# The last feed-forward tile's quantisation in two column parts, and VectorE's order in the drain

## The reference

```python
        def mx_qdq(x, s_bits=S_BITS, e_bits=E_BITS, group=GROUP):
            ...
            amax = jnp.max(jnp.abs(xg), axis=-1, keepdims=True)
            shared_exp = jnp.floor(jnp.log2(jnp.maximum(amax, tiny))) - bias
            scale = jnp.exp2(shared_exp)
            xs = xg / scale
            ...
            dq = (q * scale).reshape(shp)
        ...
        g = mx_linear(x, w_gate)
        u = mx_linear(x, w_up)
        return mx_linear(jax.nn.silu(g) * u, w_down)
```

## Time and profile before

| | |
|---|---|
| median of three runs | 700.44 us |
| the profiled execution | 700.79 us |
| its span, first to last instruction | 698.8 us |
| TensorE matmuls busy | 649.1 us (93%) |
| VectorE busy | 587.8 us (84%) |
| ScalarE busy | 509.0 us (73%) |
| GpSimd busy | 502.4 us (72%) |

### The profile page before, as it was taken

How to read it: one execution, slowest core, us unless ns; L and a number is a source line. 1 busy time by engine, 2 the same in 40 slices (tenths; PEclk the granted TensorE clock), 3 DMA queues, 4 the chain that set the end, 5 groups by cost and what they waited for, 6 DMA issues and landing times.

```text
span 698.8 us, 13988 instructions
## 1 busy us (share of the span) xinstructions
PE 649.1 (93%) x5188; PEld 340.7 (49%) x5200; DVE 587.8 (84%) x881; ACT 509.0 (73%) x969; POOL 502.4 (72%) x617
## 2 busy tenths in 40 slices
PE   0749899999999999999999999999999999999994
PEld 0749787354444443443443434434444454555542
DVE  3948977998788998988988989988889479999995
ACT  5244366878888797888888887987888756665665
POOL 1326456889898798898898987988786774767563
PEclk9857999999999999999999999999999999999999
DMA  9990202000000000001000000000000000000011
GB/s 310 163 259 21 63 3 75 1 15 17 16 16 1 32 17 15 31 1 31 31 1 31 31 1 32 4 27 28 1 13 1 1 1 1 31 30 31 32 46 75
DMA packets 21763, 26.91 MB, mean 39 GB/s; under 512 B 4032, under 2 KB 12224, under 8 KB 21696
## 3 DMA queue, kind: packets, MB, share of 16 engines
q1 hardware_dynamic: 21696, 26.02, 13.3%
HBM read 21.82 MB, written 4.19 MB: 37 GB/s over the span
## 4 chain that ended last, share of the span: by engine, by line
PE 77%; DVE 8%; issue 6%; POOL 4%; ACT 3%; DMA 2%; SPq 0%; POOLq 0%; ACTq 0%; DVEq 0%
PE banks L2470 9%; PE banks L2447 9%; PE banks L2437 9%; PE banks L2494 9%; PE banks L2480 9%; PE banks L2517 8%; PE banks L2551 7%; PE banks L2422 4%; PE banks L2578 3%; PE banks L2405 2%; PE banks L2525 2%; DMA big<-in_L_ffn_w_down_dram 2%; PE banks L2506 1%; DVE big L826 1%; PE banks L2458 1%
## 5 line engine op out<-in xcount | busy, mean ns | idle before, releaser
L1551 ACT ACTIVATE big<-banks 128x512 f32<-128x512 f32 (+3 forms) x352 | 196.6, 590 | 47.7 <-PE banks L2480 22.5
L541 POOL TENSOR_TENSOR big<-big 128x512 f32<-128x512 f32 x128 | 137.1, 1085 | 21.7 <-DVE big L931 21.6
L1621 ACT ACTIVATE big<-banks,big 128x512 f32<-128x512 f32 x128 | 87.8, 692 | 21.5 <-DVE big L911 21.4
L911 DVE TENSOR_REDUCE big<-banks 128x1 f32<-128x512 f32 x128 | 82.9, 680 | 18.2 <-PE banks L2437 16.9
L532 POOL TENSOR_TENSOR big<-big 128x512 f32<-128x512 f32 x64 | 82.2, 1285 | 15.1 <-ACT big L1626 14.8
L917 DVE TENSOR_REDUCE big<-banks 128x16 f32<-128x1024 f32 x64 | 77.4, 1209 | 17.8 <-PE banks L2447 17.4
L2470 PEld LDWEIGHTS banks<-ident,big 128*128 128x128 f32 x512 | 54.6, 141 | 76.6 <-issue 36.3
L922 DVE TENSOR_TENSOR big<-banks,big 128x1024 f32<-128x1024 f32 x64 | 78.1, 1221 | 5.5 <-PE banks L2480 3.8
L2480 PEld LDWEIGHTS banks<-ident,big 128*128 128x128 f32 x512 | 55.0, 141 | 54.2 <-ACT big L1551 28.0
L2470 PE MATMUL banks<-ident,big 128*128 128x128 f32 x512 | 79.5, 283 | 1.5 <-ACT big L1551 1.5
L2480 PE MATMUL banks<-ident,big 128*128 128x128 f32 x512 | 75.4, 282 | 0.4 <-ACT big L1551 0.3
(11 more groups left out here) (111 smaller groups left out, 1204.8 us busy)
## 6 DMA issues: line engine op xcount, KB each, us to landing
big<-in_x_dram SPq DMA_DIRECT2D x8, 1024.0 KB, 11.2
big<-in_ctx_dram SPq DMA_DIRECT2D x16, 256.0 KB, 2.9
out_dram<-big SPq DMA_DIRECT2D x16, 256.0 KB, 2.0
big<-in_L_ffn_w_down_dram SPq DMA_DIRECT2D x4, 688.0 KB, 12.0
big<-in_L_ffn_w_gate_dram SPq DMA_DIRECT2D x10, 256.0 KB, 2.7
big<-in_L_ffn_w_up_dram SPq DMA_DIRECT2D x10, 256.0 KB, 2.8
wg_area<-in_L_xattn_Wq_dram SPq DMA_DIRECT2D x2, 128.0 KB, 11.4
wg_area<-in_L_xattn_Wk_dram SPq DMA_DIRECT2D x2, 128.0 KB, 7.8
```

What stands on the lines that cost most here:

```text
L541: pool.tensor_tensor(e, e, r, ALU.mult).then_inc(s.p_ready, 1)
L911: dve.tensor_reduce(kneg[:, par, i:i + 1], bank[par], X, ALU.max, negate=True).then_inc(s.k_max_ready, 1)
L1551: return act.activation(dst, src, ACT.Copy)
L1621: act.activation(EK[:, f % 2, par, i], bank[par], ACT.Exp, bias=kneg[:, par, i:i + 1], accum_out=ksum[:, f % 2, par, i:i + 1]).then_inc(s. ...
```

## The change

The last tile (15) is quantised in two parts, columns 0 to 767 (24 groups) and 768 to 1375 (19 groups), the same cut as that of its transposes. The first part needs only two of the three column pieces of the hidden row, so its maximum is taken before the third is there. `transpose_h(15, 0)` waits for the first part alone. VectorE's list is written anew from `multiply_h(15, 1)` on.

```diff
+    LAST = [(0, 6 * P // GRP), (6 * P // GRP, FFN // GRP)]
...
+            def shift_last(r):
+                pool.wait_ge(s.h_inv_ready, T + r)
+                g0, g1 = LAST[r]
+                amax, inv, scale = (v[:, g0:g1] for v in hk[(T - 1) % 2])
+                group_scales(amax, inv, scale)
+                h = hs[:, (T - 1) % 4, GRP * g0:GRP * g1]
+                pool.tensor_tensor(groups(h), groups(h), spread(inv, g1 - g0), ALU.mult).then_inc(s.hy_ready, 1)
...
-            shift_hidden(T - 1)
+            shift_last(0)
+            shift_last(1)
...
+            def scale_last(r):
+                g0, g1 = LAST[r]
+                dve.wait_ge(s.h_ready, NC * (T - 1) + 2 + r)
...
+                dve.tensor_reduce(hk[(T - 1) % 2][0][:, g0:g1], groups(hs[:, (T - 1) % 4, GRP * g0:GRP * g1]), X, ALU.max,
+                                  apply_absolute_value=True).then_inc(s.h_max_ready, 1)
+
+            def mask_last(r):
+                g0, g1 = LAST[r]
+                dve.wait_ge(s.h_max_ready, T + r)
+                amax = hk[(T - 1) % 2][0][:, g0:g1].bitcast(I32)
+                dve.tensor_scalar(amax, amax, 0x7F800000, None, ALU.bitwise_and).then_inc(s.h_inv_ready, 1)
+
+            def clip_last(r):
+                g0, g1 = LAST[r]
+                dve.wait_ge(s.hy_ready, T + r)
+                dve.wait_ge(s.hq_ready, T - 1)
+                to_fp8(h8[:, GRP * g0:GRP * g1], hs[:, (T - 1) % 4, GRP * g0:GRP * g1]).then_inc(s.h_clipped, 1)
+
+            def dequant_last(r):
+                g0, g1 = LAST[r]
+                dve.wait_ge(s.h_clipped, T + r)
+                dve.wait_ge(s.tr_ready, tr_no[T - 3, "h1"] + 1)
+                dve.tensor_tensor(groups(hq[:, (T - 1) % 2, GRP * g0:GRP * g1]), groups(h8[:, GRP * g0:GRP * g1]),
+                                  spread(hk[(T - 1) % 2][2][:, g0:g1], g1 - g0), ALU.mult).then_inc(s.hq_ready, 1)
...
             multiply_h(T - 1, 1)
+            scale_last(0)
             add_down(T - 5)
+            mask_last(0)
             out_stats(T - 5)
             clip_hidden(T - 2)
             multiply_h(T - 1, 2)
-            scale_hidden(T - 1)
-            mask_hidden(T - 1)
+            scale_last(1)
+            mask_last(1)
             dequant_hidden(T - 2)
             add_down(T - 4)
+            clip_last(0)
+            dequant_last(0)
+            clip_last(1)
+            dequant_last(1)
+            add_down(T - 3)
             out_stats(T - 4)
-            add_down(T - 3)
-            clip_hidden(T - 1)
-            dequant_hidden(T - 1)
             out_stats(T - 3)
...
-                pe.wait_ge(s.hq_ready, u + 1)
+                pe.wait_ge(s.hq_ready, T + r if u == T - 1 else u + 1)
```

More of the change, by code:

```diff
@@ L1009, in dequant_hidden @@
                                   ).then_inc(s.hq_ready, 1)
+            def scale_last(r):
+                g0, g1 = LAST[r]
+                dve.wait_ge(s.h_ready, NC * (T - 1) + 2 + r)
+                dve.wait_ge(s.hy_ready, T - 2)
+                dve.wait_ge(s.hq_ready, T - 2)
+                dve.tensor_reduce(hk[(T - 1) % 2][0][:, g0:g1], groups(hs[:, (T - 1) % 4, GRP * g0:GRP * g1]), X, ALU.max,
[16 more added lines that the diff above has]
+                                  spread(hk[(T - 1) % 2][2][:, g0:g1], g1 - g0), ALU.mult).then_inc(s.hq_ready, 1)
             def add_down(u):
```

## The result

The changed kernel took 703.16 us, the median of six runs (702.24 to 704.41), beside 700.71 us for the kernel before (six runs, 700.11 to 701.4). The ratio is 1.0041, with a 95% interval of 1.0028 to 1.0053: 2.9 us slower, 2.0 to 3.7 (the two medians are 2.45 apart). The prediction was 702.8, in a range of 700.8 to 703.6. The profiled execution took 703.17, its span 701.4.

The account below looks back on a forecast made before the run. Two chains bound the end: tile 15's quantisation and ScalarE's copies queued behind out_prep waiting for statistics. Late statistics put down(15, 1) at 693.66 instead of 691.22, +2.4 us: 703.2 profiled, 702.8 median, range 700.8 to 703.6.

Parts of the forecast that it names:

- Part 1: VectorE up to the second part's mask: two instructions added ahead of out_stats(11) add 0.95 us; out_prep(11), copy_h(12, 1) 0.85 later.
- The prices of the parts: 768- and 608-column instructions priced on a straight line between 512- and 1376-column rows, e.g. GpSimd multiplication 1.48 and 1.21 us.
- Part 2: GpSimd beside VectorE: the first to start finishes, the other waits; last dequantisation ends at 687.2, gaining 0.25 us.
- rival 1: GpSimd's multiplications and VectorE don't hold each other up; last dequantisation ends at 685.0; +0.3 us, 700.8; chance 0.12.
- Part 3: Tile 12's statistics start at 687.75 instead of 682.40, delaying out_prep(12) and copies queued behind it on ScalarE; down(15, 1) at 693.66.
- the sum: +2.4 us at the span's end, from down(15, 1) starting at 693.66 instead of 691.22; 702.8 as median.
- The second (mask first): mask_last(1) comes ahead of GpSimd's first multiplication; last dequantisation ends at 687.6; +2.85 us, 703.3; chance 0.13.
- The third (faster): ScalarE not held by tile 12's late statistics, the end goes with the dequantisation; TensorE's 1.62 us wait goes, 698.8; chance 0.04.

Follow-up runs that it names:

- split alone: Against the kernel before: tile 15's maximum, mask, clip and dequantisation split in two, VectorE's old order kept; 701.08 us beside 700.25, ratio 1.0009.
- without meetings: Against the changed kernel: GpSimd multiplies only the first 32 columns of each part of tile 15; 700.54 us beside 700.60 for the kernel before, ratio 0.9997.
- the statistics back: Against the changed kernel: out_stats(12) moved back right behind add_down(12), ahead of clip_last(0); 701.12 us beside 700.60 for the kernel before, ratio 1.0002.
- the last version: Split kept from the changed kernel, lists of VectorE, GpSimd and ScalarE reordered against meetings and late statistics; 697.95 us beside 700.25 for the kernel before, ratio 0.9964.
- one copy ahead and its gap filled: Against the changed kernel: copy_h(14, 1) ahead of out_prep(12) on ScalarE, 13 further matmuls behind down(14, 1); 702.90 us beside 700.31 for the kernel before.
- all copies ahead: Against the changed kernel: copy_h(14, 1), copy_h(15, 0), copy_h(15, 1) ahead of out_prep(12) on ScalarE; 701.05 us beside 700.25 for the kernel before, ratio 1.0006.
- the order alone: Against the kernel before, unsplit: clip_hidden(15), dequant_hidden(15) and add_down(13) put ahead of out_stats(12); 704.42 us beside 700.60, ratio 1.0055.

## Why the prediction was right

**Part 1** (VectorE and the step to ScalarE) held. Counted from the drain's start, `copy_h(12, 1)` was put at 5.02 and came at 5.04; `mask_last(1)` at 5.79 and came at 5.84.

**The prices of the parts** held: maximum 0.96 and 0.79 (0.95 and 0.78 predicted), clip 0.55 and 0.47 (0.55, 0.46), second dequantisation 0.79 (0.79), first multiplication 1.48 (1.48), second 1.21 (1.21) where it meets nothing (split alone).

**Part 2** (the meetings) held, event by event, counted in the same way: the mask 1.31 long where it was put to end 1.33 behind its start, the dequantisation of tile 14 done 8.65 us behind the drain's start (8.62), the last dequantisation 12.81 (12.8). The 0.13 that I let the later instruction save was 0.15 for the second multiplication (it ends 1.06 behind the clip, 1.21 alone) and 0.14 for the dequantisation (0.82 behind the multiplication, 0.96 alone). The runs without meetings and with the split alone show that it is the meeting: the same instruction is long beside a long multiplication and short beside one of 32 columns. Of the rule of the Trainium skill (SBUF — State Buffer, "SBUF: two separate sides") the trace bears out both halves, the whole instruction and the one that starts first. The page limits the lock, on VectorE's side, to instructions in a two-port mode or with two inputs in SBUF, which the prediction left out. The runs agree that not every instruction takes it: clip, mask and dequantisation did, but statistics (0.69) ran beside a multiplication of 1.21 with the statistics back, and a maximum (0.79) beside one of 1.48 in the last version, none of them longer. One pair doesn't fit by its recorded starts: in the kernel before `out_rsqrt(12)`, at 684.89, took 0.98 instead of 0.55 to 0.58, and the clip that started 0.08 behind it took 0.88, its usual time. So starts less than 0.1 apart don't tell here which of two goes first.

The prediction has two figures for what the split would gain at the last dequantisation without meetings: 2.2 in part 2, and 2.5 by the 685.0 of rival 1. Both can't be; the run without meetings has 2.1 (10.9 us behind the drain's start, 13.0 before). That the end moves one for one with this dequantisation held: there it ended 1.88 earlier than in the changed kernel, and `copy_h(15, 0)` started 1.88 earlier.

**Part 3** (the statistics) held in its result and, in one respect, was put more broadly than it is. `out_prep(12)` was put 14.25 behind the drain's start and came at 14.26, `copy_h(15, 0)` 16.63 and 16.65, `copy_h(15, 1)` 18.43 and 18.45. I named two that wait, the transposes on TensorE and the copies on ScalarE; the sum went by the second. The run with one copy ahead and its gap filled shows that the first has no part in it: `transpose_h(15, 1)` was 2.6 us earlier and the drain the same 24.39. The run with all copies ahead shows that the second carries the changed kernel's loss, and that a loss of 0.76 remains without it, by the results behind the same `out_prep(12)`. The prediction didn't see what `copy_h(15, 0)` waits for once the statistics of tile 12 are in time: `out_prep(13)`, whose statistics follow the last dequantisation.

**What the sum lacked** is TensorE's clock. I let matmuls behind a gap cost what they cost before. In the profiled execution they ran at half speed for about 3.0 us, from 689.66 to 692.6, which is the 0.27 us between the 2.46 that the steps give and the 2.73 seen. That the time came out in the range doesn't bear on this term: it is smaller than the interval of the ratio. In the drain of before nothing showed it: there the longest wait ahead of tile 15 was 1.62 us, and five matmuls behind the next gap took 1.26. The kernel's start showed that the granted clock does fall: from 30 to 40 us TensorE was busy 4.57 us of 10, and the granted clock was 0.50.

**The rivals.** The first (meetings don't count) would have needed a mask of 0.18; it was 1.31. Its price, +0.3, was low: the run without meetings had a drain 0.58 longer. The second (mask first) would have needed a longer first multiplication; it had its 1.48. The third (faster) would have needed `out_prep(12)` by 684.6; it was at 688.49.

## What to carry to other kernels

Where each engine runs a fixed list, ask of every step that is moved back who waits for it, and what is queued behind that waiter: here a 0.9 us pair of instructions, put five microseconds later, cost more than the split could give. A long multiplication of GpSimd should run beside VectorE's reductions and statistics, not beside its clips, masks and dequantisations: the shift's 16 multiplications took 2.50 to 2.51 us beside the former, and a mask or a dequantisation met by a multiplication took 0.9 to 1.3 us longer. With the lists written by both rules the kernel with the split is 2.5 us faster than before, though no run tells the split's share in that. And look at where TensorE's idle time ends up: a gap of 3.09 us just ahead of its last eleven matmuls cost 1.85 us on top of itself here, by the clock.

## What the runs showed of the hardware that I had not expected

TensorE's granted clock is at 0.50 (1.2 of 2.4 GHz) behind a gap of 2.75 us in one execution of the changed kernel and at 1.00 behind the same gap in another. Behind the gap of 3.09 us it stayed at 0.50 for all eleven remaining matmuls, 4.87 us. In the run of the order alone TensorE waited 1.65 us, ran six transposes at 1.00, waited 2.06 us, and was at 0.50 behind that. With the gap filled by matmuls it was 1.00 in both kernels. What decides between the two executions of the changed kernel is open.
